# A causal mask of turned scores moved from PE to POOL in the second attention of a five-part hybrid network

## The reference

```python
x = _L0_conv_ref(x, ...)      # non-local block with batch norm
x = _L1_conv_ref(x, ...)      # quantised convolutions
t = _to_tokens(x)             # [8, 256 tokens, 256]
t = t + _L2_attn_ref(_ln_t(t), ...)    # attention, ALiBi bias, causal, 16 heads of 16
t = t + _L2_ffn_ref(_ln_t(t), ...)     # ternary weights
t = t + _L3_attn_ref(_ln_t(t), ...)    # attention, causal, 16 heads of 16
t = t + _L3_ffn_ref(_ln_t(t), ...)     # 8 experts, the two best of each token
x = _from_tokens(t, x)
```

```python
scores = jnp.einsum('bhqd,bhkd->bhqk', q, k) / jnp.sqrt(d_k)
causal = jnp.tril(jnp.ones((t, t), dtype=bool))
scores = jnp.where(causal, scores, -jnp.inf)
attn = jax.nn.softmax(scores, axis=-1)
y = jnp.einsum('bhqk,bhkd->bhqd', attn, v)
```

## Time and profile before

| | |
|---|---|
| median of 3 runs | 669.19 us (667.11 to 670.29) |
| the profiled execution's own time | 668.89 us |
| its span, first to last instruction | 666.4 us |
| PE busy | 592.3 us, 4159 instructions |
| DVE busy | 447.5 us, 1275 |
| ACT busy | 326.2 us, 548 |
| POOL busy | 117.9 us, 115 |
| granted clock of PE, mean | 0.966 of 2.4 GHz |

### The profile page before, as it was taken

One profiled execution on the slowest core, in us unless ns is written; L12 is line 12 of the kernel. 1 busy time (PEld: TensorE's weight loads), 2 busy tenths in 40 slices (PEclk: granted clock), 3 DMA queues, 4 the chain that ended last, 5 costly groups with the idle time before them and its releaser, 6 DMA issues.

```text
span 666.4 us, 11227 instructions
## 1 busy us (share of the span) xinstructions
PE 592.3 (89%) x4159; PEld 407.4 (61%) x4206; DVE 447.5 (67%) x1275; ACT 326.2 (49%) x548; POOL 117.9 (18%) x115
## 2 busy tenths in 40 slices
PE   5884876767899999999999989999999999999897
PEld 2743434645667767777777767566675756565443
DVE  4668858727676686685785676776858667675464
ACT  2336658615666666665666554344443535353110
POOL 2021000242223233223123122011020200000000
PEclk9986898796999999999999999999999999999999
DMA  9400000499684593584483481608053170000000
GB/s 336 213 0 0 1 0 6 82 149 147 81 148 85 64 146 82 67 140 90 63 142 81 65 143 42 101 17 142 2 112 47 55 105 17 1 17 0 17 12 20
DMA packets 40253, 50.64 MB, mean 76 GB/s; under 512 B 4052, under 2 KB 33492, under 8 KB 39892
## 3 DMA queue, kind: packets, MB, share of 16 engines
q1 hardware_dynamic: 40200, 49.94, 40.3%
HBM read 35.11 MB, written 14.68 MB: 75 GB/s over the span
## 4 chain that ended last, share of the span: by engine, by line
PE 59%; DVE 15%; issue 3%; ACT 2%; DMA 2%; SPq 1%; POOL 0%; DVEq 0%; ACTq 0%
PE ps L1252 14%; PE ps L1135 8%; PE ps L1127 8%; PE ps L1209 5%; PE ps L1198 5%; DVE nmax L1419 4%; PE ps L1119 3%; PE ps L1194 3%; PE ps L1178 3%; PE ps L1170 3%; PE ps L1216 2%; DVE acc L1499 2%; PE ps L1173 2%; DVE xn L1375 2%; DVE stats L1364 2%
## 5 line engine op out<-in xcount | busy, mean ns | idle before, releaser
L1419 DVE TENSOR_REDUCE nmax<-ps 128x2 f32<-128x512 f32 (+1 forms) x192 | 130.9, 687 | 75.9 <-PE ps L1178 48.1
L1312 ACT ACTIVATE PT<-ps 128x512 f32<-128x512 f32 x192 | 113.4, 598 | 116.3 <-PE ps L1198 114.7
L1252 PE MATMUL ps<-wm,xnT 128*128 128x512 f32 x256 | 119.9, 599 | 0.7
L1079 POOL TENSOR_TENSOR rstd<-ve,fix 128x2 f32<-128x2 f32 x32 | 22.2, 695 | 323.8 <-DVE ve L1370 323.8
L1306 ACT ACTIVATE QS<-ps 8x1024 bf16<-8x1024 f32 x64 | 65.1, 1017 | 26.3 <-PE ps L1183 24.2
L1198 PE MATMUL ps<-QS,KS 110*128 110x256 bf16 (+3 forms) x512 | 74.5, 247 | 0.0
L1499 DVE SCALAR_TENSOR_TENSOR acc<-ps,gate,acc 128x256 f32<-128x256 f32 x128 | 61.6, 482 | 18.5 <-PE ps L1252 16.2
L1252 PEld LDWEIGHTS ps<-wm,xnT 128*128 128x128 f32 x256 | 45.1, 190 | 39.7 <-issue 38.1
L1127 PE MATMUL ps<-xnT,by_dim 128*128 128x256 f32 x256 | 63.9, 397 | 2.2 <-ACT xnT L1277 2.2
L1099 POOL TENSOR_TENSOR parts<-rest,fix 128x512 bf16<-128x512 f32 x30 | 38.1, 1271 | 140.3 <-DVE rest L1388 97.5
L1194 PE MATMUL ps<-fixb 128*128 128x256 bf16 (+1 forms) x192 | 59.9, 312 | 2.3 <-DVE nmax L1419 2.0
(11 more groups left out here) (211 smaller groups left out, 913.7 us busy)
## 6 DMA issues: line engine op xcount, KB each, us to landing
parts_dram<-parts SPq DMA_DIRECT2D x32, 384.0 KB, 3.3
QS<-parts_dram SPq DMA_DIRECT2D x96, 128.0 KB
KS<-parts_dram SPq DMA_DIRECT2D x96, 128.0 KB, 7.9
wt<-wt_dram SPq DMA_DIRECT2D x1, 2562.0 KB, 18.6
wm<-wm_dram SPq DMA_DIRECT2D x1, 2449.0 KB, 13.2
xc<-x_dram SPq DMA_DIRECT2D x8, 256.0 KB, 5.4
out_dram<-res SPq DMA_DIRECT2D x8, 256.0 KB, 2.1
w<-w_dram SPq DMA_DIRECT2D x1, 845.0 KB, 7.7
```

The lines of the kernel that those rows point to most:

```text
L1252: mm = pe.matmul(d, normT(stage, batch)[:, c, t * P:(t + 1) * P], M("We", c * EXPERTS * CH + e * 2 * CH, 2 * CH), start=(c == 0), stop=(c ...
L1312: act.activation(PT[:, pt_slot(piece, n), :], bank(piece), ACT.Exp).then_inc(drain(piece), 1)
L1419: dve.tensor_reduce(group[:, 0, :] if part == 0 else group[:, 1, 2 * part - 2:2 * part], bank(piece).rearrange("p (j n) -> p j n", n=w_), ...
```

## The change

In stage 2 the mask matmul of X is left out; each score matmul then opens and closes its own columns of PSUM. ACT's exponential is as before, now of unmasked scores. POOL then takes the masked columns of the unit in PT, bounds them by 3e38 (an unmasked exponential may be infinite, and infinity times zero isn't a number), waits for itself, and multiplies them in place by `keep`, a tile of ones and zeros [128, 128] broadcast over the heads. O0 and O1 wait for `masked` in stage 2 instead of for ACT. `keep` is made once at the block's start: PE turns the triangle into a free bank, DVE compares it with zero. The first attention keeps its mask on PE.

```diff
--- before.py
+++ after.py
@@ -34,6 +34,7 @@
 SQRT2 = 1.4142135
 EPS = 1e-5
 MASKED = -1e30
+LARGEST = 3e38
 QUARTERS = (2, 0, 3, 1)
 
 
@@ -174,7 +175,7 @@
     if kind in SETTLED:
         out.append(("dve_step", settled(piece)))
     out += {"LNa": [("var_ready", 1), ("rstd_ready", 1)], "LNb": [("xn_ready", 1)], "XB": [("x_biased", 1)],
-            "MS": [("max_split", 1)], "PAD": [("own_rows", 1), ("padded", 4), ("chosen", 1), ("chosen_spread", 16 * (STACKS - 1))], "CT": [("out_stored", 16)],
+            "MS": [("max_split", 1)], "X": [("bounded", 1), ("masked", 1)] if piece[1] == 2 else [], "PAD": [("own_rows", 1), ("padded", 4), ("chosen", 1), ("chosen_spread", 16 * (STACKS - 1))], "CT": [("out_stored", 16)],
             "Q": [("first_ready0", 1)], "K": [("first_ready1", 1)],
             "SPLIT": [(f"second_ready{n}", 1), (f"third_ready{n}", 1), (f"parts_stored{n}", 16)],
             "LOAD": [(f"stack_loaded{n}", 16 * (len(Q_PARTS) + (piece[1] == 0 and n == 0)))],
@@ -966,6 +967,7 @@
             res = lb("res", [P, 2, NC2, PIX])
 
             sems = {name: sem(name) for name in COUNTS.total}
+            keep = lb("keep", [P, P])
             prepared = sem("prepared")
             bias_turned = sem("bias_turned")
             bias_loaded = sem("bias_loaded")
@@ -1085,6 +1087,16 @@
                         .then_inc(sems["x_biased"], 1)
                 if kind == "SPLIT" and (stage, batch) != (0, 0):
                     split(pool, piece)
+                if kind == "X" and stage == 2:
+                    if piece == ("X", 2, 0, 0):
+                        pool.wait_ge(prepared, 4)
+                    drained(pool, piece)
+                    heads = 4 if n % 3 == 2 else 2
+                    weights = PT[:, pt_slot(piece, n), :].rearrange("p (j n) -> p j n", j=heads)[:, :, 0:P]
+                    pool.tensor_scalar(weights, weights, LARGEST, None, ALU.min).then_inc(sems["bounded"], 1)
+                    wait(pool, "bounded", piece)
+                    pool.tensor_tensor(weights, weights, keep[:].unsqueeze(1).broadcast_to([P, heads, P]), ALU.mult)\
+                        .then_inc(sems["masked"], 1)
 
             def split(eng, piece):
 
@@ -1119,6 +1131,13 @@
                             mm = pe.transpose(d[:, c * PIX + t * P:c * PIX + (t + 1) * P],
                                               src[:, t, c * P:(c + 1) * P], F("ident"))
                     return mm
+
+                def weighed(unit):
+
+                    if stage == 2:
+                        wait(pe, "masked", unit)
+                    else:
+                        drained(pe, unit)
 
                 def rows(w, src):
 
@@ -1191,17 +1210,18 @@
                     heads = (0, 1) if part == 0 else (2, 3) if part == 1 else (0, 1, 2, 3)
                     kt = part // 2
                     width = 512 // len(heads)
-                    pe.matmul(d.rearrange("p (j n) -> p j n", n=width)[:, :, 0:P], FB("tri0", 0, P),
-                              FB("ident").unsqueeze(1).broadcast_to([P, len(heads), P]), start=True, stop=False,
-                              skip_group_check=True)
+                    if stage == 0:
+                        pe.matmul(d.rearrange("p (j n) -> p j n", n=width)[:, :, 0:P], FB("tri0", 0, P),
+                                  FB("ident").unsqueeze(1).broadcast_to([P, len(heads), P]), start=True, stop=False,
+                                  skip_group_check=True)
                     for k, j in enumerate(heads):
                         mm = pe.matmul(d[:, k * width:(k + 1) * width], KS[r, at, 4 * g + j, kt * P:(kt + 1) * P],
-                                       QS[r, at, 4 * g + j, kt * P:], start=False, stop=(k == len(heads) - 1),
-                                       skip_group_check=True)
+                                       QS[r, at, 4 * g + j, kt * P:], start=(stage == 2), stop=(stage == 2 or k == len(heads) - 1),
+                                       skip_group_check=(stage == 0))
                 if kind == "O0":
                     o = ps[:, 6 + n % 2, :]
-                    drained(pe, ("X", stage, batch, 3 * n))
-                    drained(pe, ("X", stage, batch, 3 * n + 1))
+                    weighed(("X", stage, batch, 3 * n))
+                    weighed(("X", stage, batch, 3 * n + 1))
                     if n == 0:
                         drained(pe, ("V", stage, batch, 0))
                     drained(pe, ("O1", stage, batch, n), 1)
@@ -1211,7 +1231,7 @@
                                   start=True, stop=False, skip_group_check=True)
                 if kind == "O1":
                     o = ps[:, 6 + n % 2, :]
-                    drained(pe, ("X", stage, batch, 3 * n + 2))
+                    weighed(("X", stage, batch, 3 * n + 2))
                     for j in range(4):
                         mm = pe.matmul(o[32 * j:32 * j + 32, P:PIX], V[:, at, 1, 4 * n + j, :],
                                        PT[:, pt_slot(piece, 3 * n + 2), j * P:(j + 1) * P],
@@ -1522,6 +1542,8 @@
 
                 @block.tensor
                 def _(pe):
+                    pe.wait_ge(fixb_loaded, 16)
+                    pe.matmul(ps[:, 7, P:2 * P], FB("tri0", 0, P), FB("ident"), start=True, stop=True)
                     pe.wait_ge(prepared, 1)
                     both = WT["bq0"][0]
                     pe.matmul(ps[:, 7, 0:2 * NC2], ident_by_dim[:], wt[:, both:both + 2 * NC2], start=True, stop=True)\
@@ -1545,7 +1567,8 @@
                     dve.wait_ge(bias_turned, 1)
                     dve.tensor_scalar(qk_bias[:, 0], ps[:, 7, 0:NC2], DH ** -0.5, None, ALU.mult).then_inc(prepared, 1)
                     dve.tensor_copy(qk_bias[:, 1], ps[:, 7, NC2:2 * NC2]).then_inc(prepared, 1)
-                    dve.wait_ge(prepared, 3)
+                    dve.tensor_scalar(keep[:], ps[:, 7, P:2 * P], 0.0, None, ALU.is_equal).then_inc(prepared, 1)
+                    dve.wait_ge(prepared, 4)
                     for piece in in_order("others"):
                         vector_piece(dve, piece)
```

## The result

The changed kernel takes 683.45 us (median of 4 runs, 681.76 to 684.99) against 669.74: a ratio of 1.0215, 95% interval 1.0181 to 1.0248. The profiled execution took 682.15 us, with a span of 680.4.

A forecast was written before the change was run, and what follows sets the result against it. PE, busy 89% of the span, was taken as the bound. Images 2 to 4 -1.5 us, 5 to 7 -4.4, 0 and 1 +3.1, start +0.3: total -2.5, 666.4 us, or 666.7 as median; range 657 to 678.

The forecast's parts named there:

- the matmuls' worth: PE, second attention: removing the mask matmuls frees 14.1 us by their starts, 1.76 us per image.
- the bound's price: POOL, each unit: the one-input bound takes 0.60 us for 512 columns and 0.33 for 256.
- the port: Shared SBUF port: POOL instructions hold DVE's two-operand steps; 0.9 + 0.35 us per image in 2 to 4, 0.3 in 5 to 7.
- Rival 3: POOL bounds images 0 and 1 (+9.6 us) if the bound costs as much as the product: +7.2, 676.4 us; chance 0.24.
- rival 1: POOL's bound runs at the memset's rate, 0.45 and 0.25 us: -5.5 us in all, 663.7 us; chance 0.14.
- paid back in full: PE: a matmul taken away returns its whole time where nothing new becomes late; 1.76 us per image.
- weren't there to take is excluded by the starts: PE, second attention: start-to-start times were said to rule out that the matmuls' 14.1 us could not be gained.
- O0 and O1: PE, second attention: these wait for POOL instead of ACT, expected to show only around images 0 to 2.
- The start of the stage: Block's start: one more small DVE step and the wait between two, +0.3 us.

The follow-up runs named there:

- the run with powers: Changed kernel with POOL's bound and product replaced by similarly long powers on few columns, PE not waiting for POOL, mask missing from output: 673.67 us, ratio 1.0060.
- the run with a tile of its own: Changed kernel with POOL's bound and product done on a separate tile, O0 and O1 waiting for ACT, mask missing from output: 683.40 us, ratio 1.0216.
- with select: Changed kernel with one POOL affine_select in place of bound and product, in all eight images: 665.75 us, ratio 0.9952 to the kernel before.

## Why the prediction was wrong

- **The result** lies past the range's upper end (678). Against the forecast, by stretch: images 0 and 1 +9.4 us instead of +3.1, images 2 to 4 +4.0 instead of -1.5, images 5 to 7 +0.3 instead of -4.4 (the third transpose of xn, forecast with image 4, counts in image 5 there). The mechanisms were named; three terms of the sum had the wrong size: the matmuls' worth, the bound's price and the port.
- **Rival 3**, held at 0.24, saw the way it went. Its +9.6 for images 0 and 1 fits the measured 9.4 partly by luck: it had units of 22.1 us per image and 2 us more in which POOL would yield the port. No run shows such yielding (the split's product takes 1.27 us in both kernels), and the units by themselves came to 24, those 2 us more. The 7 us that its 676.4 is short lie in images 2 to 7. Its neighbour, rival 1, has a slip: with the prices given, the units add up to 15.6 us per image, not 15.2.
- **The matmuls' worth.** The starts give 14.1 us and each matmul did go (a narrow unit lasts 0.22 us instead of 0.33). The step that failed is "paid back in full": I put 1.76 us per image in the sum for images 2 to 7. The run without a mask has 0.9 to 1.1 in images 3 to 7, and 6.5 us in all: waits for xn, attn and attnT came forward to meet it. That the 14.1 us "weren't there to take is excluded by the starts" was wrong: the starts show what a matmul takes from PE, not what the kernel gets back. The earlier trace rows showed PE 98.7% busy, but the earlier trace rows named a wait of the transposes.
- **The bound's price.** I took 0.60 and 0.33 us with 1.27 and 0.65 as the upper end. It is 1.49 and 0.85, above that end: this one-input operation was no cheaper than the two-input one. With the product of 0.73 for 256 columns (0.65 taken) the units come to 24 us per image and POOL's load to 30 against 25.5. That is the largest miss: images 0 and 1 at +3.1 forecast and +9.4 measured. Without a mask they gain 1.0 us, and the full queue of the run with powers takes 10.0. The Trainium skill's line in "GPSIMD Engine Reference", section "When to use GPSIMD", that one-input operations are roughly line-rate, does not hold for this bound: 512 columns took 1486 ns. Select, also with one input, is nearer to it: 641 ns, and 0.9 ns for each further column.
- **The port.** The mechanism was right: L1375 as L1395, the nparts steps and ve were held, nmax wasn't, and the transpose of xn at the end of image 3 waited for 2.0 us, where 1.0 to 1.1 was forecast. Its size was not, and I spread it evenly where the steps differ: 9.7 us, some 1.6 of them image 4's low clock. The sum had 0.9 + 0.35 per image in 2 to 4 and 0.3 in 5 to 7; images 3, 5, 6 and 7 show 1.5, 1.4, 1.0 and 1.0 us between powers and bound with product. For images 6 and 7 it is the router's step and `acc` behind it, which the sum didn't have.
- **O0 and O1** waited for POOL in images 0 and 1 only, as forecast, and by the run with a tile of its own the wait as such cost nothing: without it PE waited for xn instead.
- **The start of the stage** (+0.3 in the sum): no cost can be seen. The first exponential of the first attention starts at 157.0 us before and at 155.8 after, and between those two in the other traces.
- **The clock** wasn't in the sum. Behind PE's long idle in images 0 and 1 it fell to half for 6.8 us at 398 and 3.4 us at 411 (already image 2), and again at 490 after the 2.0 us of idle; before it stayed at 1.00 from 160 us to the end of these stages. The same 2.0 us of idle at 450 and 531 were followed by no fall. Image 4's extra 1.6 us over image 3 go with the fall at 490. What the two others cost isn't separated from the queue; the run without a mask has 3.4 us of low clock at 402 too.

## What to carry to other kernels

Work that is moved to an idle engine is priced by what that engine's instructions do to the others: here POOL's product held DVE's small two-operand steps, the cast of nparts and xn until it ended, half an xn by 0.9 us, and select held the nparts steps in the same way. Take the shortest single instruction (select: 0.41 us for what bound and product did in 1.57), and look first at the held steps that the bounding engine waits for, here xn and the sum `acc`. Before counting a matmul's full time as gain, delete it and time that alone: here it was 6.5 us of 14.1. In a kernel whose stretches differ, add up the new load stretch by stretch: 39 us had room for it, 25 did not.

## What the runs showed of the hardware

- POOL's TENSOR_SCALAR min in f32 took 847 ns for 256 columns and 1486 for 512, TENSOR_TENSOR mult 726 and 1267, AFFINE_SELECT 409 and 641; a power took 698 ns for 2 columns, 850 for 3, 1322 for 6, 1481 for 7, about 0.155 us per column.
- DVE's nparts, ve, router steps and xn were held by POOL's product to its end, by select too (0.51 us of nparts under a select of 0.64); the bound held them only for 0.1 to 0.4 us (nparts at 486.34 took 0.56 us and was through 0.85 us before the bound ended), and the powers not at all: DVE's busy time was 449.0 us beside 304 us of POOL. Not held beside the product: nmax (687 ns) and `acc`, which read PSUM, but also the statistics of the normalisation (L1384, 0.41 to 0.42 us) and the router's reduction (L1480, 0.17 us), from SBUF to SBUF.
- More than halving POOL's masking work (no bound: 188.8 to 87.5 us) raised the mean hold on nparts from 0.33 to 0.56 us over its 0.17: the moment of the start counted for more than the load. And a held step isn't a lost one: with select nparts was held for the same 0.33 us in the mean, the splits' part included, at a cost of at most 0.3 to 0.4 us per image.
